# Where the split operands of a decoder layer begin within a 16-byte line of SBUF, and one projection made in half-width products

## The chip, the cores and the metric

The kernel runs on one core of a Trainium2 chip. The metric is the device time of one execution in microseconds; the kernel before takes 2354.44 us as the median of three runs (2353.5 to 2355.1). A forecast is compared with that median.

## The reference, cut to what matters

Sixteen batches of 512 tokens with 512 channels pass through one decoder layer, all in float32:

```
qkv = einsum('btc,ec->bte', x, Wqkv) + bqkv          # 512 -> 3 x 512
q, k = elu(q * scale) + 1, elu(k * scale) + 1
y = q * cumsum(k * v) / clip(einsum over a head(q, cumsum(k)), 0.001)
x = layernorm(x + y @ Wproj.T + bproj)
x = layernorm(x + channel_attention(x, ctx_1024))     # 4 heads of 128 channels, twice
e = argmax(mean over tokens(x) @ Wr + br)             # one expert of 8 per batch
h = relu(x @ W1[e] + b1[e])                           # 512 -> 2048
x = layernorm(x + h @ W2[e] + b2[e])                  # 2048 -> 512
```

## The kernel before

TensorE multiplies in the type float32r. To keep float32 accuracy, each float32 operand is split in SBUF into a high part (ScalarE copies it into a float32r tensor) and a low part (VectorE subtracts the high part from the original). A product of two matrices then takes three products: high by high, high by low, low by high. In each one operand is stationary (128 x 128, loaded by an LDWEIGHTS before every product) and the other moves past it (128 rows, 512 columns, 2048 bytes in each partition).

Four places make nearly all products:

- **The projections q, k and v** (`by_high` L1045 to L1049 and `qkv` L1051 to L1080). A batch has 12 jobs (3 kinds x 4 blocks of 128 channels). A job walks over the four channel tiles t of the input; at each t two products take xT_hi as moving operand (high and low weights, L1049) and one takes xT_lo (L1079). That makes 12 x 4 x 3 = 144 products for a batch, 2304 for all. Batch 1 uses x2T_hi and x2T_lo in place of xT_hi and xT_lo.
- **The output projection** (`project`, L1117 to L1119): 4 x 4 x 3 = 48 products for a batch. Here xT_hi and xT_lo (after the attention they hold y) are stationary and the weights wp_hi and wp_lo move.
- **The expert's first layer** (`up`, L1250 to L1252): for each of 16 blocks of the hidden width, 4 x 3 = 12 products into one PSUM bank. The weights we_hi and we_lo are stationary, x2T_hi and x2T_lo move: 192 products for a batch, 3072 for all.
- **The expert's second layer** (`down`, L1274, and for the last four blocks `down_last`, L1290): again 12 products for each block. The hidden parts h_hi and h_lo are stationary, the weights we_hi and we_lo move: 192 for a batch, 3072 for all.

The remaining products (the Gram matrix of x and the context, transposes, token sums) are plain float32 with 128 or fewer columns; they don't use the split tensors.

Each engine's order is fixed by a table of time slots: `JOB`, `DEN`, `FFN` and their like give for each step of the work the half-step at which an engine issues it. The batches overlap, so that projections and attention of later batches stand between the expert blocks of an earlier one. `up` of a block stands three half-steps ahead of its `down`; in between ScalarE makes hid and h_hi (L561, L568) and VectorE h_lo (L921). Semaphores, all written by hand, order the engines against each other.

In the beginning `qkv(0, 0, 0)` waits at each channel tile t for xhi_done and xlo_done, that is for ScalarE's xT_hi (L658) and VectorE's xT_lo (L1010) of that tile. Before it, `keep_busy` issues some products without a use.

All tensors are allocated one behind the other. In the built program each of them begins at a multiple of 16 bytes in its partition, and the slices that TensorE reads are multiples of 512 bytes into them, so that no operand of a product begins anywhere else than at the start of a 16-byte line. The lines that the change touches:

```
xT_hi, xT_lo = sb("xT_hi", [P, CC, T], F32R), sb("xT_lo", [P, CC, T], F32R)
x2T_hi, x2T_lo = sb("x2T_hi", [P, CC, T], F32R), sb("x2T_lo", [P, CC, T], F32R)
h_hi, h_lo = sb("h_hi", [P, 2, T], F32R), sb("h_lo", [P, 2, T], F32R)
```

h_hi has a second use: for batches 0 and 1 it holds the high and low weights of projection job 11, which SyncE also stores to DRAM once (L279).

Of the kernel before, what the change touches and what calls it, by code (L numbers as in the profile page):

```python
# [6 lines left out]
F32R = mybir.dt.float32r  # L7
# [5 lines left out]
P = 128  # L13
NB = 16
T = 512
C = 512
CC = C // P
# [82 lines left out]
def build(nc, d, out):  # L100
    wq_dram = nc.dram_tensor("wq_scratch", [JOBS, P, 2 * CC * P], F32, kind="Internal").ap()

    with ExitStack() as ctx:
        def sb(name, shape, dt=F32):
            return ctx.enter_context(nc.sbuf_tensor(name, shape, dt))
# [8 lines left out]
        raw_q = raw[:, :, :].rearrange("p r (s n) -> p (r s) n", s=2)  # L114
        diag = sb("diag", [P, 2, XH, P], F32R)
        xT_raw = sb("xT_raw", [P, CC, T])
        xT_hi, xT_lo = sb("xT_hi", [P, CC, T], F32R), sb("xT_lo", [P, CC, T], F32R)
        x2T_hi, x2T_lo = sb("x2T_hi", [P, CC, T], F32R), sb("x2T_lo", [P, CC, T], F32R)
        h_hi, h_lo = sb("h_hi", [P, 2, T], F32R), sb("h_lo", [P, 2, T], F32R)
        hid = sb("hid", [P, 2, T])  # L120
        rden_all = sb("rden_all", [P, T], F32R)
        head_all = sb("head_all", [P, CC, P], F32R)
# [10 lines left out]
        aT = sb("aT", [P, XH, P])  # L133
        const_b = sb("const_b", [P, C])
        x_sum = sb("x_sum", [P, C])

        ident, ones, ones_r = sb("ident", [P, P]), sb("ones", [P, P]), sb("ones_r", [P, P], F32R)
        head_sum = sb("head_sum", [P, CC, SEG])
# [79 lines left out]
        def bank(a, j):  # L218
            return (acc if a == 1 or a == 2 and j < EARLY else AB)[j % 2]
# [820 lines left out]
        def _(pe):  # L1040
            def keep_busy(bank, n):
                for _ in range(n):
                    pe.matmul(bank[:, 0:P], ones[:, :], ones[:, :], start=True, stop=True)

            def by_high(a, j, t):  # L1045
                w = held(j if a < 2 else j % NQ).rearrange("p (s t n) -> p s t n", s=2, t=CC)
                x_hi = x2T_hi if a == 1 else xT_hi
                for s in range(2):
                    pe.matmul(bank(a, j)[:, :], w[:, s, t, :], x_hi[:, t, :], start=(t == 0 and s == 0), stop=False)  # L1049

            def qkv(a, cc, part):  # L1051
                j = 3 * cc + part
                if a == 0:
                    pe.wait_ge(wqhi_done, j + 1)
                    pe.wait_ge(wqlo_done, j + 1)
                if a > 1:
                    pe.wait_ge(wq_in[j % NQ], 16 * (CC * (a - 2) + cc + 1))

                if part == 0 and cc > 0:
                    pe.wait_ge(kv_done, CC * a + cc)  # L1060
                if part == 1 and cc > 0:
                    pe.wait_ge(eq_done, 2 * CC * a + 2 * cc)
                if part == 2:
                    pe.wait_ge(ek_done, 2 * CC * a + 2 * cc + 2)
                if a == 2 and j < 2:
                    pe.wait_ge((kv_done, eq_done)[j], (2 * CC, 4 * CC)[j])
                n = j - EARLY if a == 2 else j
                if n in (0, 1) and a > 1:
                    pe.wait_ge(res1_done, TT * a - n)
                    pe.wait_ge(x2lo_done, CC * (a - 2) + 2 + n)  # L1070
                w = held(j if a < 2 else j % NQ).rearrange("p (s t n) -> p s t n", s=2, t=CC)
                x_lo = x2T_lo if a == 1 else xT_lo
                for t in range(CC):
                    if j == 0 and (a == 0 or t % 2 == 0):
                        pe.wait_ge(xhi_done, t + 1 if a == 0 else 2 * a + t // 2 + 3)
                        pe.wait_ge(xlo_done, t + 1 if a == 0 else 2 * a + t // 2 + 3)
                    if not ahead(a, j, t):
                        by_high(a, j, t)
                    last = pe.matmul(bank(a, j)[:, :], w[:, 0, t, :], x_lo[:, t, :], start=False, stop=(t == CC - 1))  # L1079
                last.then_inc(JOB_MM[part], 1)  # L1080

            def denominator(a):
# [333 lines left out]
```

## Time and profile before

| what | value |
|---|---|
| median of three runs | 2354.44 us (2353.5 to 2355.1) |
| profiled execution, first to last instruction (span) | 2352.2 us |
| TensorE busy with products | 2332.6 us, 99% |
| TensorE busy with weight loads (beside products) | 1927.6 us, 82% |
| VectorE busy | 1652.7 us, 70% |
| ScalarE busy | 1144.1 us, 49% |
| GpSimd busy | 451.6 us, 19% |
| mean granted clock of TensorE | 0.998 of full speed |

The span is the profiled execution's own time from its first to its last instruction; the page gives no other time for it. The median of the unprofiled runs lies 2.2 us above it, which covers what lies around the span and the spread from run to run.

How to read it: the products are pipelined, so the mean duration of one (389 ns for 512 columns) is not what it costs. What it costs is the distance from its start to the start of the next. A busy share of 99% therefore says that TensorE hardly ever ran dry, not that its products could not be closer together. The distance is read from the timeline, in which rows that have several products ("x2") begin with the first of them.

### The profile page before, as it was taken

Reading aid. Unit: us, or ns where it says so; the run is one execution under the profiler, and the core shown is the slowest. Engines: PE = TensorE matmul, PEld = TensorE weight load, DVE = VectorE, ACT = ScalarE, POOL = GpSimd, SP = SyncE. Lnnn points to the kernel's source line nnn. Section 1 sums busy time; section 2 is a strip of 40 time slices with the busy share of each in tenths; the row PEclk is TensorE's granted clock in tenths of the full one; section 3 lists DMA queues with packets and bytes.
Section 4 is the critical chain, followed back from the end, with each engine's and each line's share of the span. In section 5 each row is a group of like instructions: output and inputs, shape, how many; then the busy total and the mean of one; then the engine's idle time right before and its main releaser. Section 6 shows DMA issues by size and latency. Waiting matters only on the chain.

```text
span 2352.2 us, 34307 instructions
## 1 busy us (share of the span) xinstructions
PE 2332.6 (99%) x12060; PEld 1927.6 (82%) x12060; DVE 1652.7 (70%) x2863; ACT 1144.1 (49%) x1902; POOL 451.6 (19%) x395
## 2 busy tenths in 40 slices
PE   9999999999999999999999999999999999999998
PEld 7878888888888888888888888888888888888787
DVE  8886685866858668586675867758677586875643
ACT  5354445454454544545455444545454454554543
POOL 1112211121121212212122111211113111121200
PEclk9999999999999999999999999999999999999999
DMA  9255445463444634446354454544536435453332
GB/s 341 83 160 188 117 144 163 133 218 106 150 155 143 207 102 179 132 144 206 108 182 133 138 193 126 187 127 143 180 117 206 117 135 179 126 161 99 100 116 90
DMA packets 97276, 354.77 MB, mean 151 GB/s; under 512 B 11858, under 2 KB 11986, under 8 KB 86994
## 3 DMA queue, kind: packets, MB, share of 16 engines
q1 hardware_dynamic: 80210, 319.02, 38.2%
q0 software_dynamic: 16896, 33.56, 9.0%
q8 instruction: 98, 1.61, 0.3%
q14 instruction: 72, 0.59, 0.1%
HBM read 329.47 MB, written 23.07 MB: 150 GB/s over the span
## 4 chain that ended last, share of the span: by engine, by line
PE 92%; DVE 1%; ACT 1%; issue 1%; POOL 0%; DMA 0%; SPq 0%; POOLq 0%; DVEq 0%; ACTq 0%
PE acc L1274 29%; PE m L1049 13%; PE h_ps L1250 10%; PE h_ps L1252 10%; PE h_ps L1251 10%; PE m L1079 6%; PE m L1133 2%; PE m L1210 2%; PE m L1117 2%; PE m L1118 2%; PE m L1119 2%; PE m L1231 1%; PE m L1090 1%; PE m L1103 1%; PE acc L1290 0%
## 5 line engine op out<-in xcount | busy, mean ns | idle before, releaser
L561 ACT ACTIVATE hid<-h_ps,b 128x512 f32<-128x512 f32 x252 | 173.6, 689 | 598.2 <-PE h_ps L1252 597.5
L1049 PE MATMUL m<-xT_hi,wq 128*128 128x512 f32 x1320 | 408.2, 390 | 0.3 <-DVE xT_lo L1010 0.3
L1250 PE MATMUL h_ps<-x2T_hi,we_hi 128*128 128x512 f32 x1008 | 400.4, 397 | 2.4 <-DVE x2T_lo L905 2.4
L1274 PE MATMUL acc<-we_hi,h_hi 128*128 128x512 f32 x1008 | 400.8, 398 | 1.5 <-DVE h_lo L921 1.5
L921 DVE TENSOR_TENSOR h_lo<-hid,h_hi 128x512 fp32r<-128x512 f32 x252 | 224.3, 890 | 252.9 <-ACT h_hi L568 252.9
L1252 PE MATMUL h_ps<-x2T_hi,we_lo 128*128 128x512 f32 x1008 | 392.9, 390 | 0.0
L1274 PE MATMUL acc<-we_hi,h_lo 128*128 128x512 f32 x1008 | 392.8, 390 | 0.0
L1274 PE MATMUL acc<-we_lo,h_hi 128*128 128x512 f32 x1008 | 392.7, 390 | 0.0
L1251 PE MATMUL h_ps<-x2T_lo,we_hi 128*128 128x512 f32 x1008 | 392.4, 389 | 0.0
L911 DVE TENSOR_TENSOR we_lo<-raw,we_hi 128x1024 fp32r<-128x1024 f32 x256 | 319.9, 1250 | 31.2 <-ACT we_hi L551 31.2
L499 ACT ACTIVATE e_f<-m,sb_qkv,scale 128x512 f32<-128x512 f32 x116 | 90.5, 780 | 479.8 <-PE m L1079 477.7
L1049 PEld LDWEIGHTS m<-xT_hi,wq 128*128 128x128 f32 x1320 | 246.7, 188 | 51.3 <-ACT xT_hi L658 0.7
L551 ACT ACTIVATE we_hi<-raw 128x1024 fp32r<-128x1024 f32 x256 | 267.9, 1046 | 6.7 <-DMA raw<-in_w 6.3
L1079 PE MATMUL m<-xT_lo,wq 128*128 128x512 f32 x660 | 257.0, 389 | 0.0
L1250 PEld LDWEIGHTS h_ps<-x2T_hi,we_hi 128*128 128x128 f32 x1008 | 189.3, 188 | 43.5 <-issue 4.1
L1274 PEld LDWEIGHTS acc<-we_hi,h_hi 128*128 128x128 f32 x1008 | 189.4, 188 | 41.3 <-issue 3.0
L1274 PEld LDWEIGHTS acc<-we_hi,h_lo 128*128 128x128 f32 x1008 | 189.2, 188 | 40.3
L1252 PEld LDWEIGHTS h_ps<-x2T_hi,we_lo 128*128 128x128 f32 x1008 | 189.2, 188 | 40.2
L1251 PEld LDWEIGHTS h_ps<-x2T_lo,we_hi 128*128 128x128 f32 x1008 | 189.4, 188 | 37.1
L1274 PEld LDWEIGHTS acc<-we_lo,h_hi 128*128 128x128 f32 x1008 | 189.5, 188 | 36.8
L568 ACT ACTIVATE h_hi<-hid 128x512 fp32r<-128x512 f32 x252 | 159.5, 633 | 8.0
L1079 PEld LDWEIGHTS m<-xT_lo,wq 128*128 128x128 f32 x660 | 123.9, 188 | 26.0
(259 smaller groups left out, 3368.6 us busy)
## 6 DMA issues: line engine op xcount, KB each, us to landing
raw<-in_w SPq DMA_DIRECT2D x256, 512.0 KB, 4.2
wq<-wq_scratch SPq DMA_DIRECT2D x168, 512.0 KB, 3.3
x<-in_x_tok SPq DMA_DIRECT2D x16, 1024.0 KB, 5.5
x<-in_b_proj POOLq DMA_DIRECT2D x16, 1024.0 KB, 14.7
ctx_T<-in_ctxT SPq DMA_DIRECT2D x16, 1024.0 KB, 8.2
x<-in_b POOLq DMA_DIRECT2D x16, 1024.0 KB, 11.8
ctx_tok<-in_ctx_tok SPq DMA_DIRECT2D x15, 1024.0 KB, 4.7
out_dram<-x SPq DMA_DIRECT2D x15, 1024.0 KB, 4.8
```

The costliest lines, as they stand in the source:

```text
L499: act.activation(e_f[:, :], ps[:, :], ACT.Exp, bias=sb_qkv[:, col:col + 1], scale=scale[:, 0:1]).then_inc(done, 1)
L551: act.activation(we_hi[:, g % NW, :], raw[:, g % NR, :], ACT.Copy).then_inc(whi_done, 1)
L561: act.activation(hid[:, f % 2, :], up_bank(b, f)[:, :], ACT.Relu, bias=b1[:, b % 2, f:f + 1]).then_inc(h_done, 1)
L568: act.activation(h_part(h_hi, xT_hi, b, f), hid[:, f % 2, :], ACT.Copy).then_inc(hhi_done, 1)
L911: dve.tensor_tensor(we_lo[:, g % NW, :], raw[:, g % NR, :], we_hi[:, g % NW, :].bitcast(F32), ALU.subtract).then_inc(wlo_done, 1)
L921: dve.tensor_tensor(h_part(h_lo, xT_lo, b, f), hid[:, f % 2, :], h_part(h_hi, xT_hi, b, f).bitcast(F32), ALU.subtract).then_inc(hlo_done, 1)
L1049: pe.matmul(bank(a, j)[:, :], w[:, s, t, :], x_hi[:, t, :], start=(t == 0 and s == 0), stop=False)
L1079: last = pe.matmul(bank(a, j)[:, :], w[:, 0, t, :], x_lo[:, t, :], start=False, stop=(t == CC - 1))
L1250: pe.matmul(ps, we_hi[:, g % NW, js], x2T_hi[:, j, :], start=(j == 0), stop=False)
L1251: pe.matmul(ps, we_hi[:, g % NW, js], x2T_lo[:, j, :], start=False, stop=False)
L1252: last = pe.matmul(ps, we_lo[:, g % NW, js], x2T_hi[:, j, :], start=False, stop=(j == CC - 1))
L1274: last = pe.matmul(acc[t][:, :], hx[:, f % 2, ts], wx[:, g % NW, C:], start=(f == 0 and n == 0), stop=(f == FC - 1 and n == 2))
```

## The change

The six split tensors x2T, h and xT (high and low each) are no longer allocated by themselves. They are slices of one tensor `split` of 4 + 4 x 4 x 512 + 4 x 512 words in each partition, whose own start is a multiple of 16 bytes. x2T_hi and x2T_lo begin one word (4 bytes) past a 16-byte line, h_hi and h_lo two words (8 bytes), xT_hi and xT_lo three words (12 bytes). Every slice of them that an engine reads or writes keeps that offset, since all steps within them are multiples of 512 bytes. The tensors that stood behind them (from hid to x_sum) move down in the partition by multiples of 512 bytes; the small ones behind `split` move up by 32 bytes.

The second part: job 0 of batch 0 (`a == 0 and j == 0`) is made of products of 256 columns, two in place of each one of 512. That takes 24 products and 24 weight loads in place of 12.

```diff
-        xT_hi, xT_lo = sb("xT_hi", [P, CC, T], F32R), sb("xT_lo", [P, CC, T], F32R)
-        x2T_hi, x2T_lo = sb("x2T_hi", [P, CC, T], F32R), sb("x2T_lo", [P, CC, T], F32R)
-        h_hi, h_lo = sb("h_hi", [P, 2, T], F32R), sb("h_lo", [P, 2, T], F32R)
...
+        split = sb("split", [P, 4 + 4 * CC * T + 4 * T], F32R)
+
+        def part(words, n, tiles):
+            return split[:, words + n * tiles * T:words + (n + 1) * tiles * T].rearrange("p (c t) -> p c t", c=tiles)
+
+        x2T_hi, x2T_lo = part(1, 0, CC), part(1, 1, CC)
+        h_hi, h_lo = part(2 + 2 * CC * T, 0, 2), part(2 + 2 * CC * T, 1, 2)
+        xT_hi, xT_lo = part(3 + 2 * CC * T + 4 * T, 0, CC), part(3 + 2 * CC * T + 4 * T, 1, CC)
...
+            def columns(a, j):
+                return (slice(0, T // 2), slice(T // 2, T)) if a == 0 and j == 0 else (slice(0, T),)
+
             def by_high(a, j, t):
...
                 for s in range(2):
-                    pe.matmul(bank(a, j)[:, :], w[:, s, t, :], x_hi[:, t, :], start=(t == 0 and s == 0), stop=False)
+                    for n, ns in enumerate(columns(a, j)):
+                        pe.matmul(bank(a, j)[:, ns], w[:, s, t, :], x_hi[:, t, ns], start=(t == 0 and s == 0 and n == 0), stop=False)
...
-                    last = pe.matmul(bank(a, j)[:, :], w[:, 0, t, :], x_lo[:, t, :], start=False, stop=(t == CC - 1))
+                    for ns in columns(a, j):
+                        last = pe.matmul(bank(a, j)[:, ns], w[:, 0, t, :], x_lo[:, t, ns], start=False,
+                                         stop=(t == CC - 1 and ns.stop == T))
```

The order of instructions differs in one place only, on TensorE in the beginning of the program. Before, jobs 0 and 1 of batch 0 stand there so (m is the PSUM bank, wq the weights):

```order
L1043 MATMUL m<-ones 128x128
L1049 MATMUL m<-xT_hi,wq 128x512 x2
L1079 MATMUL m<-xT_lo,wq 128x512
L1049 MATMUL m<-xT_hi,wq 128x512 x2
L1079 MATMUL m<-xT_lo,wq 128x512
```

In the changed kernel the same place on TensorE reads so, where `split` is the tensor that holds all six parts:

```order
L1048 MATMUL m<-ones 128x128
L1058 MATMUL m<-split,wq 128x256 x4
L1089 MATMUL m<-split,wq 128x256 x2
L1058 MATMUL m<-split,wq 128x256 x4
L1089 MATMUL m<-split,wq 128x256 x2
L1058 MATMUL m<-split,wq 128x256 x4
L1089 MATMUL m<-split,wq 128x256 x2
L1058 MATMUL m<-split,wq 128x256 x4
L1089 MATMUL m<-split,wq 128x256 x2
L1058 MATMUL m<-split,wq 128x512 x2
L1089 MATMUL m<-split,wq 128x512
```

Each of the four channel tiles of job 0 has six products in place of three. From job 1 on (the last two rows), and on VectorE, ScalarE, GpSimd and SyncE throughout, as many instructions stand in the same order as before, with the same shapes.

## Rows read from the trace of the kernel before

**Rows 1.** The page: span, busy time by engine, chain that ended last.
```profile
span 2352.2 us, 34307 instructions
PE 2332.6 (99%) x12060; PEld 1927.6 (82%) x12060; DVE 1652.7 (70%) x2863; ACT 1144.1 (49%) x1902; POOL 451.6 (19%) x395
...
PE 92%; DVE 1%; ACT 1%; issue 1%; POOL 0%; DMA 0%; SPq 0%; POOLq 0%; DVEq 0%; ACTq 0%
```

**Rows 2.** Groups by form: count, busy us, mean ns, idle us before with releaser.
```profile
L1049 PE MATMUL m<-xT_hi,wq 128*128 128x512 f32 x1320 | 408.2, 390 | 0.3 <-DVE xT_lo L1010 0.3
L1274 PE MATMUL acc<-we_hi,h_hi 128*128 128x512 f32 x1008 | 400.8, 398 | 1.5 <-DVE h_lo L921 1.5
L1250 PE MATMUL h_ps<-x2T_hi,we_hi 128*128 128x512 f32 x1008 | 400.4, 397 | 2.4 <-DVE x2T_lo L905 2.4
...
L1251 PE MATMUL h_ps<-x2T_lo,we_hi 128*128 128x512 f32 x1008 | 392.4, 389 | 0.0
```

**Rows 3.** Timeline of TensorE (start us, us, instruction), projections of batch 0.
```profile
16.18 0.61 PE L1049 MATMUL m<-xT_hi,we_hi 128*128 128x512 f32 x2
...
36.58 0.61 PE L1049 MATMUL m<-xT_hi,we_lo 128*128 128x512 f32 x2
```

**Rows 4.** Timeline of TensorE in the middle: Gram, a second and a first expert layer.
```profile
1001.20 3.73 PE L1133 MATMUL m<-ctx_tok,x 128*128 128x128 f32 x32
...
1005.46 0.39 PE L1274 MATMUL acc<-we_hi,h_hi 128*128 128x512 f32 x1
...
1007.28 0.39 PE L1274 MATMUL acc<-we_hi,h_lo 128*128 128x512 f32 x1
...
1010.22 0.39 PE L1250 MATMUL h_ps<-x2T_hi,we_hi 128*128 128x512 f32 x1
...
1011.81 0.39 PE L1251 MATMUL h_ps<-x2T_lo,we_hi 128*128 128x512 f32 x1
```

**Rows 5.** By stretch: us, busy of PE, PEld, DVE, ACT, POOL; granted clock.
```profile
40.00:47.80 7.80, 5.91 (x53) 4.28 (x51) 7.64 (x11) 4.17 (x6) 0.00 (x0) 1.00 1.07 265
47.80:54.60 6.80, 6.09 (x12) 3.77 (x13) 6.78 (x11) 5.22 (x10) 0.00 (x0) 0.50 0.96 399
```

**Rows 6.** Timeline of TensorE within that second stretch.
```profile
48.16 1.22 PE L1103 MATMUL m<-rden_all,head_all 128*128 128x512 f32 x2 [2.25 <-ACT rden_all L627]
...
53.39 0.63 PE L1118 MATMUL m<-wp_lo,xT_hi 128*128 128x512 f32 x1
53.81 0.63 PE L1119 MATMUL m<-wp_hi,xT_lo 128*128 128x512 f32 x1
```

**Rows 7.** Weight loads by form.
```profile
L1133 PEld LDWEIGHTS m<-ctx_tok,x 128*128 128x128 f32 x480 | 55.9, 192 | 1.2
...
L1250 PEld LDWEIGHTS h_ps<-x2T_hi,we_hi 128*128 128x128 f32 x1008 | 189.3, 188 | 43.5 <-issue 4.1 <-DVE x2T_lo L905 1.7
```

**Rows 8.** Timeline of TensorE, job 0 and the beginning of job 1.
```profile
6.50 0.86 PE L1049 MATMUL m<-xT_hi,wq 128*128 128x512 f32 x2
...
7.44 0.62 PE L1049 MATMUL m<-xT_hi,wq 128*128 128x512 f32 x2
...
8.59 0.70 PE L1049 MATMUL m<-xT_hi,wq 128*128 128x512 f32 x2 [0.30 <-DVE xT_lo L1010]
...
10.04 0.62 PE L1049 MATMUL m<-xT_hi,wq 128*128 128x512 f32 x2
```

**Rows 9.** Groups of VectorE and ScalarE that write the split tensors.
```profile
L921 DVE TENSOR_TENSOR h_lo<-hid,h_hi 128x512 fp32r<-128x512 f32 x252 | 224.3, 890 | 252.9 <-ACT h_hi L568 252.9
L905 DVE TENSOR_TENSOR x2T_lo<-m,x2T_hi 128x512 fp32r<-128x512 f32 x62 | 40.0, 685 | 61.6 <-ACT x2T_hi L540 61.6
L753 DVE TENSOR_TENSOR xT_lo<-ctx_tok,xT_hi 128x512 fp32r<-128x512 f32 x60 | 38.5, 686 | 20.9 <-ACT xT_hi L522 20.9
...
L568 ACT ACTIVATE h_hi<-hid 128x512 fp32r<-128x512 f32 x252 | 159.5, 633 | 8.0
```

## The prediction

> **What bounds the kernel now.** I read the page first: of a span of 2352.2 us TensorE is busy for 2332.6, and the chain that ended last lies on it for 92% [rows 1]. The groups by form come next, to see what TensorE ever waits for: the first product of a block in the expert's first layer was late by 2.4 us in all, that of the second layer by 1.5 us, that of the projections by 0.3 us [rows 2]. So there is nearly no wait to remove, and no other engine's time matters unless it grows a lot. What counts is the distance between the starts of products.
>
> That distance is in the timeline. From 16.18 to 36.58 us there are thirty groups of three products without a gap: 20.40 / 90 = 0.2267 us for one product of 512 columns [rows 3]. The middle of the program has the same: 8 distances in 1.82 us in the second layer and 7 in 1.59 us in the first, 0.227 us each [rows 4]. At 2.4 GHz 512 columns are 213.3 ns. Each product thus costs 13.3 ns more than its columns (32 cycles), whichever stage it stands in and whatever the others do meanwhile. In a stretch with the clock granted at half, 1.2 GHz [rows 5], the distance is 53.81 - 53.39 = 0.42 us [rows 6], and 512 columns at 1.2 GHz are 426.7 ns: there the extra is gone. So the 13.3 ns don't look like a fixed price of an instruction, but like something that shows only when words are wanted at the full rate. Loading weights doesn't set the distance: a load takes 188 ns and is hidden, with 43.5 us of idle time before the 1008 loads of one group, and in the Gram matrix 32 products, each with a load of its own, stand (3.73 - 0.27) / 31 = 0.112 us apart, the last one's own length of about 0.27 us taken off [rows 4, 7].
>
> **The change, part by part.** *Where the moving operand begins.* xT and x2T move in the projections (12 jobs x 4 tiles x 3 products x 16 batches = 2304) and in the first expert layer (16 blocks x 12 x 16 = 3072): 5376 products whose 2048 bytes begin 4 or 12 bytes past a line and so touch 129 lines where 128 were touched. The second expert layer and the output projection move weights, which stay where they were. In the trace every operand begins at a line, so the price of the offset stands nowhere and needs bounds. Upper end: the stream falls to one word for each cycle at 1.2 GHz, the 426.7 ns that the half clock shows [rows 6], which is 200 ns more for each, 5376 x 0.2 = 1075 us. Lower end: the offset takes away what makes the 13.3 ns, 5376 x 13.3 ns = 72 us less. Between them lies one more line: 213.3 ns for 128 lines are 1.67 ns a line, and 226.7 / 128 = 1.77 ns; at most 5376 x 1.77 = 9.5 us. I take nothing for it. The nearest row to an uneven stream is a product at the full clock, and its distance is the same in all stages although the weight slices and the work of ScalarE and VectorE beside it vary; the reading seems to be fetched ahead, and one fetch more at the ends of 512 columns can fall into the 13.3 ns between them.
>
> On this point there is a rule that speaks against the change. The Trainium skill, page "SBUF — State Buffer", section "Specifications (TRN2)", says that SBUF is read in lines of 16 bytes, that two hits on a line are needed for the full rate and that each step to a new line costs something. A product that begins 12 bytes past a line has one hit on its first line, one that begins 4 bytes past it has one hit on its last. No row here shows it. If the rule holds as a price for each line, the sum is the +9 us of the first rival below; if it is only about single hits, it is less.
>
> *Where the stationary operand begins.* h is stationary in the second expert layer (3072) and xT or x2T in the output projection (48 x 16 = 768); h_hi as weights of job 11 adds 24. A load reads 512 bytes, 33 lines in place of 32. It ends 227 - 188 = 39 ns ahead of the next one's start [rows 3, 7], so it could become a fifth longer unseen: nothing. Were that cover gone, 3864 loads at one line each (at most 188 / 32 = 5.9 ns) would be 23 us. Below nothing, if the 13.3 ns came from loads that meet the moving stream: a further 3864 x 13.3 ns = 51 us less.
>
> *VectorE and ScalarE.* They write all six parts and VectorE reads the high ones again. Their durations now are 633 to 890 ns [rows 9]. VectorE's mean for h_lo is 890 ns where the same operation takes 685 for x2T_lo [rows 9]; so it is already drawn out by 0.2 us in the mean, and TensorE has waited only 1.5 us for it in 2352 [rows 2]. An odd start that cost a few cycles, or even again 0.2 us, is hidden behind the three half-steps between the two expert layers: nothing. The lower bound is nothing too, since faster helpers shorten no wait above 4.2 us in all (2.4 + 1.5 + 0.3). If the cover were gone, with 0.2 us for each of the 256 h_lo exposed, it would be 51 us; the engine is busy for 70% only, and I don't see it.
>
> *Halves in job 0 of batch 0.* 12 products become 24. One of 256 columns takes at least half of 226.7 ns, 113.3, which is also about the 112 ns at which products with their own load follow each other [rows 4]; at most as long as a whole one, 226.7. With a fixed 13.3 ns it would be 120, and this I take: 24 x 120 - 12 x 226.7 = +160 ns, with ends of 0 and +2.7 us. A part of it lies beside a wait: at 8.59 us TensorE stands 0.30 us for VectorE's xT_lo, and the first tiles are apart by 7.44 - 6.50 and 8.59 - 7.44 us, more than three products need [rows 8]. Behind the third tile TensorE doesn't wait again until job 1 at 10.04 us, so only two tiles' extra of 80 ns moves what follows. Queued behind are the jobs of batch 0, and VectorE and ScalarE wait for those, not the reverse.
>
> *Sum* against the profiled execution: 2352.2 + 0 + 0 + 0 + 0.1 = 2352.3 us of span. The median of the runs is 2.2 us above the span, which gives 2354.5. As several of the small prices above can only add, and hardly one of them is negative, I forecast 2355. The case's own range is 2353 to 2358.
>
> **The rivals.**
> 1. *An extra line is paid.* This is the case on the other side, slower: one mechanism, in the projections and the first expert layer, at the seam between two products. If TensorE's reading of a stream is bound by lines (1.77 ns each at 226.7 / 128), 129 lines cost 228.4 ns, and 5376 x 1.77 = +9.5 us: 2364. It decides once the price is above 0.9 ns for a product (4.7 us). For it: the extra shows only at the full clock, so the stream does run at its limit there [rows 3, 6]. Against: 32 cycles between products would be room for one fetch. With half a line, 0.8 ns, it would be +4.5 us: 2359, at the edge.
> 2. *The stream loses its rate.* If the words are fetched in pairs or fours that must not cross a line, and a crossing one takes twice: 226.7 ns becomes between 320 (half of the fetches double) and 427 ns, + 0.5 to 1.1 ms: 2860 to 3430. For it: at 2.4 GHz a word each 0.42 ns has to come, twice the rate at which the half clock asks for words [rows 6]. Against: nothing in the trace, as no operand is off its line; I hold a fetch by whole lines to be likelier.
> 3. *The extra of 13.3 ns goes away.* If it comes from stationary and moving operand beginning at the same place of a line, then all 9216 products with a part of `split` gain it: 2354 - 9216 x 13.3 ns = 2232; if for the moving ones alone, 2283. For it: the extra vanishes at the half clock, where both streams ask for less [rows 6], and every product pairs one shifted operand with one at a line. Against: 4 to 12 bytes keep both streams in nearly the same lines, and the extra is the same over all slices of the weights [rows 3, 4].
>    The Trainium skill, page "TensorE: Matmul & The Clock Gate", section "Part 2: What happens when you issue a matmul", gives TensorE two read ports that don't disturb each other, which would exclude this rival; it also gives a distance of N / 2.4 + 2.5 ns, 216 ns for 512 columns, and there the trace differs: 226.7.
> 4. *The clock.* TensorE idled 2.25 us for rden_all up to 48.16, and the clock stood at half from 47.8 to 54.6, with 6.09 us of work in it [rows 5, 6]. Should the shift of 0.1 us at the start move that stretch, up to half of the work, 3 us, comes or goes. It is inside the range.
>
> **How the numbers follow.** No change: 0.48. Rival 1: 0.26, a third of it below the point at which it can be told. Rival 2: 0.12. Rival 3: 0.09. The clock and mixtures: 0.05. What a measurement of this kernel can tell from no change is about 0.2%, 4.7 us. Within it: 0.48 + 0.09 + 0.01 = 0.58. Slower: 0.17 + 0.12 + 0.03 = 0.32. Faster: 0.09 + 0.01 = 0.10. The time is that of the likeliest case, 2355. The range leaves out rival 2 and most of rival 3, together 0.2; it holds rival 1 with some of a longer load on top, up to 2372, and a partial gain (a tenth of rival 3) down to 2342.
>
> **What would show it.** In the timeline of the changed kernel: products of the first expert layer and of the projections 226.7 ns apart as before (right), 228 (rival 1), over 300 (rival 2), about 214 (rival 3). The second expert layer keeps 226.7 ns in every case but rival 3, and its loads 188 ns. The 24 products of job 0 should stand 120 ns apart once the third tile has begun; 113 would say that the extra goes with the columns. VectorE's h_lo may be longer, but TensorE's idle time before the expert layers should stay below 5 us. The forecast is wrong if any distance of 512-column products changes by more than 0.9 ns.

## The result, and the profile after: slower by 2%

The changed kernel takes 2401.15 us (median of 4 runs, 2400.22 to 2401.72), the kernel before 2354.44 beside it (median of three, 2353.5 to 2355.1): a ratio of 1.0199, with a 95% interval of 1.0185 to 1.0214. A fourth execution of the kernel before took 8350.22 us and is left out of this comparison. The changed kernel is clearly slower; the interval leaves open whether by a little more or a little less than 2%. The forecast was 2355 us, with a range of 2342 to 2372. So 46 us have come that it did not see. The page of the profile after [rows 1]:

```profile
span 2399.1 us, 34331 instructions
PE 2379.6 (99%) x12072; PEld 1934.9 (81%) x12072; DVE 1651.1 (69%) x2863; ACT 1143.7 (48%) x1902; POOL 452.2 (19%) x395
...
PE 96%; DVE 2%; ACT 1%; issue 1%; POOL 0%; DMA 0%; SPq 0%; POOLq 0%; DVEq 0%; ACTq 0%
```

The span grew by 46.9 us and TensorE's busy time by 47.0, with 12 products and 12 loads more. VectorE and ScalarE have kept their sums to within 2 us. TensorE is "99% busy" as before: from this page alone the loss can't be told from work. The groups of the profile after (count, busy us, mean ns, idle us before them) answer to [rows 2, 7, 9]:

```profile
L1261 PE MATMUL h_ps<-split,we_hi 128*128 128x512 f32 x1008 | 410.3, 407 | 2.2 <-DVE split L910 2.2
L1058 PE MATMUL m<-split,wq 128*128 128x512 f32 x1312 | 408.4, 392 | 0.0
L1262 PE MATMUL h_ps<-split,we_hi 128*128 128x512 f32 x1008 | 402.3, 399 | 0.0
L1285 PE MATMUL acc<-we_lo,split 128*128 128x512 f32 x1008 | 395.7, 393 | 0.0
...
L1261 PEld LDWEIGHTS h_ps<-split,we_hi 128*128 128x128 f32 x1008 | 189.7, 188 | 49.8 <-issue 4.0
...
L926 DVE TENSOR_TENSOR split<-hid,split 128x512 fp32r<-128x512 f32 x256 | 224.0, 875 | 283.6 <-ACT split L573 283.6
```

TensorE waited 2.2 us for VectorE in the first expert layer where it had waited 2.4, h_lo takes 875 ns where it took 890, the loads take 188 ns as before. What grew is one product: 407 and 399 ns in the first layer (397 and 389 before), 393 in the second, where the group of we_lo and h_hi had 390. The distances behind that are in the timeline (start us, us, instruction) of the kernel after, in the middle of the program, beside [rows 4]:

```profile
1016.07 0.40 PE L1261 MATMUL h_ps<-split,we_hi 128*128 128x512 f32 x1
...
1017.50 0.64 PE L1058 MATMUL m<-split,wq 128*128 128x512 f32 x2
...
1024.07 0.39 PE L1285 MATMUL acc<-we_lo,split 128*128 128x512 f32 x1
...
1026.37 0.39 PE L1285 MATMUL acc<-we_hi,split 128*128 128x512 f32 x1
...
1029.34 0.40 PE L1261 MATMUL h_ps<-split,we_hi 128*128 128x512 f32 x1
...
1032.18 0.40 PE L1152 MATMUL m<-diag,ones_r 128*128 128x512 f32 x1
```

Six products of the first layer lie between 1016.07 and 1017.50: 0.238 us each, and twelve between 1029.34 and 1032.18: 0.237. Ten distances of the second layer lie between 1024.07 and 1026.37: 0.230. Before they were 0.227 in both [rows 4]. In the projections of batch 0 (timeline of the kernel after, against [rows 3]) it is 60 products in 13.73 us, 0.2288 us each:

```profile
16.20 0.62 PE L1058 MATMUL m<-split,we_hi 128*128 128x512 f32 x2
...
29.93 0.62 PE L1058 MATMUL m<-split,we_lo 128*128 128x512 f32 x2
```

The table below is worked out from all pairs of consecutive starts in each trace that lie under 262 ns apart (some 9000 a trace); the experiments' kernels are told below. Mean distance in ns:

| kernel | first expert layer | second | projections | output projection | ratio to before (95%) |
|---|---|---|---|---|---|
| before | 227.3 | 227.4 | 227.1 | 226.7 | |
| after | 237.2 | 230.8 | 229.8 | 228.6 | 1.0199 |
| e2_place | 227.4 | 227.6 | 227.0 | 226.8 | 1.0005 (0.9996 to 1.0015) |
| e3_x2_only | 237.9 | 228.7 | 228.3 | 228.0 | 1.0162 (1.0145 to 1.0179) |
| e4_h_only | 227.7 | 231.0 | 227.2 | 226.8 | 1.0050 (1.0033 to 1.0066) |
| e6_x_only | 228.1 | 227.8 | 229.3 | 227.2 | 1.0042 (1.0025 to 1.0059) |
| e7_whole_line | 231.5 | 228.5 | 228.0 | 228.1 | 1.0079 (1.0062 to 1.0096) |
| e8_halves_only | 227.5 | 227.6 | 227.0 | 226.8 | 1.0006 (0.9996 to 1.0015) |
| e10_x2_256_bytes | 227.3 | 227.5 | 227.0 | 226.8 | 1.0000 (0.9991 to 1.0010) |
| e11_h_36_words | 227.4 | 228.7 | 227.5 | 226.8 | 1.0026 (1.0016 to 1.0036) |
| e12_all_36_words | 232.1 | 232.2 | 233.1 | 226.9 | 1.0180 (1.0166 to 1.0194) |

The second row against the first accounts for the loss: 3072 x 9.9 ns = 30.4 us in the first layer, 3072 x 3.4 = 10.4 in the second, 2304 x 2.7 = 6.2 in the projections, 768 x 1.9 = 1.5 in the output projection, together 48.5. Two small things of these two executions stand beside it. TensorE waited 0.91 us for the third tile of job 0 and began it at 9.22 us, where it had been 8.59 [rows 8]: +0.6. The half-width products alone don't do this: in e8 that tile began at 8.57 us. And less was done at the half clock, by the windows of the profile after (columns as in [rows 5]):

```profile
51.20:54.60 3.40, 3.30 (x8) 2.21 (x8) 3.40 (x7) 2.80 (x7) 0.00 (x0) 0.50 0.59 248
```

TensorE worked 3.30 us at half speed where it had been 6.09 [rows 5]: that gives back half of 2.8, 1.4 us. The sum is 47.7 against 46.9 of span.

### The profile page after: what moved, and what is told of

The parts are those of the page before. It is cut to its first block, busy times and chain, and to the rows that moved or that the text cites. A ratio compares the mean times of both kernels' runs of the same rounds, so it can differ in the third digit from the quotient of the medians.

```text
span 2399.1 us, 34331 instructions
## 1 busy us (share of the span) xinstructions
PE 2379.6 (99%) x12072; PEld 1934.9 (81%) x12072; DVE 1651.1 (69%) x2863; ACT 1143.7 (48%) x1902; POOL 452.2 (19%) x395
## 4 chain that ended last, share of the span: by engine, by line
PE 96%; DVE 2%; ACT 1%; issue 1%; POOL 0%; DMA 0%; SPq 0%; POOLq 0%; DVEq 0%; ACTq 0%
PE acc L1285 28%; PE m L1058 13%; PE h_ps L1261 10%; PE h_ps L1263 10%; PE h_ps L1262 10%; PE m L1089 7%; PE m L1128 2%; PE m L1129 2%; PE m L1130 2%; PE m L1144 2%; PE m L1221 2%; PE m L1242 1%; PE acc L1058 1%; PE m L1101 1%; PE m L1114 1%
## 5 line engine op out<-in xcount | busy, mean ns | idle before, releaser
L1285 PE MATMUL acc<-we_hi,split 128*128 128x512 f32 x2016 | 677.9, 397 | 1.2 <-DVE split L926 1.2
L1285 PEld LDWEIGHTS acc<-we_hi,split 128*128 128x128 f32 x2016 | 379.1, 188 | 87.2 <-issue 3.0
L926 DVE TENSOR_TENSOR split<-hid,split 128x512 fp32r<-128x512 f32 x256 | 224.0, 875 | 283.6 <-ACT split L573 283.6
L1261 PE MATMUL h_ps<-split,we_hi 128*128 128x512 f32 x1008 | 410.3, 407 | 2.2 <-DVE split L910 2.2
L1058 PE MATMUL m<-split,wq 128*128 128x512 f32 (+1 forms) x1328 | 411.2, 391 | 0.9 <-DVE split L1015 0.9
L1263 PE MATMUL h_ps<-split,we_lo 128*128 128x512 f32 x1008 | 402.7, 399 | 0.0
L1262 PE MATMUL h_ps<-split,we_hi 128*128 128x512 f32 x1008 | 402.3, 399 | 0.0
L1285 PE MATMUL acc<-we_lo,split 128*128 128x512 f32 x1008 | 395.7, 393 | 0.0
L1058 PEld LDWEIGHTS m<-split,wq 128*128 128x128 f32 x1328 | 247.6, 188 | 55.5 <-ACT split L663 1.1
L1089 PE MATMUL m<-split,wq 128*128 128x512 f32 (+1 forms) x664 | 257.5, 389 | 0.0
L1261 PEld LDWEIGHTS h_ps<-split,we_hi 128*128 128x128 f32 x1008 | 189.7, 188 | 49.8 <-issue 4.0
L1263 PEld LDWEIGHTS h_ps<-split,we_lo 128*128 128x128 f32 x1008 | 191.3, 190 | 47.2
L1262 PEld LDWEIGHTS h_ps<-split,we_hi 128*128 128x128 f32 x1008 | 192.0, 190 | 44.1
L1089 PEld LDWEIGHTS m<-split,wq 128*128 128x128 f32 x664 | 124.3, 188 | 27.5
L522 ACT ACTIVATE x<-x,shift,rstd 128x512 f32<-128x512 f32 x188 | 138.0, 809 | 13.3 <-POOL shift L409 10.1
## 6 DMA issues: line engine op xcount, KB each, us to landing
x<-in_b POOLq DMA_DIRECT2D x16, 1024.0 KB, 11.8
```

Source lines behind the costliest of these rows:

```text
L522: act.activation(x[:, t, :], x[:, t, :], ACT.Identity, bias=shift[:, n, t:t + 1], scale=rstd[:, n, t:t + 1]).then_inc((x1_done, x2_done, n ...
L926: dve.tensor_tensor(h_part(h_lo, xT_lo, b, f), hid[:, f % 2, :], h_part(h_hi, xT_hi, b, f).bitcast(F32), ALU.subtract).then_inc(hlo_done, 1)
L1058: pe.matmul(bank(a, j)[:, ns], w[:, s, t, :], x_hi[:, t, ns], start=(t == 0 and s == 0 and n == 0), stop=False)
L1089: last = pe.matmul(bank(a, j)[:, ns], w[:, 0, t, :], x_lo[:, t, ns], start=False, stop=(t == CC - 1 and ns.stop == T))
L1261: pe.matmul(ps, we_hi[:, g % NW, js], x2T_hi[:, j, :], start=(j == 0), stop=False)
L1262: pe.matmul(ps, we_hi[:, g % NW, js], x2T_lo[:, j, :], start=False, stop=False)
```

## The experiments

All whole kernels are the changed kernel with other places for the parts and, but for e8, with job 0 in whole products, unless said otherwise, and every ratio is to the kernel before, run beside it on the same chip (2354.1 to 2354.4 us). e1, e5 and e9 leave the layer out and are one execution each. The expectations speak of three theories: a product pays where its own operand begins within a 16-byte line, and shifts by whole lines are free (A); the place of one operand against the other counts (B); the traffic of ScalarE and VectorE beside TensorE is needed (C).

**e1_pairs: both operands' offsets by themselves.** The layer is left out; TensorE alone does blocks of 32 products like the kernel's, each block with its own pair of offsets in words (m for the moving, s for the stationary operand), a plain product between blocks:

```
pe.matmul(bank[:, 0:n], still[:, s + j * P:s + j * P + P], moving[:, m + j * T:m + j * T + n], ...)   # j = i // 3 % 4
```

> Leaves the whole layer out (the output is a copy of x). TensorE alone: blocks of 32 float32r products, each with its own weight load, nothing beside them. The start of the moving operand and that of the stationary one are stepped through 0, 1, 2, 3, 4, 5, 6 and 8 words, all 64 pairs, and then 16, 32, 64 words for one of them, then 256 and 384 columns. Theory A (a price for each product that begins within a 16-byte line): 226.7 ns where both begin at 0, 4 or 8 words, about 237 ns where the moving operand is 1 word off, about 229 where it is 3 off, and 230 where the stationary one is 2 off. Theory B (the distance of the two streams decides, since the weights of the next product are read while this one moves): equal shifts of both (1,1), (2,2), (3,3) cost nothing, and shifts by whole lines (4, 8, 16 words of one of them) cost as well. Theory C (it needs the traffic of ScalarE and VectorE on the same tensors): all 64 pairs at 226.7 ns. For 256 columns a fixed extra gives 120 ns, an extra for each column 113 ns.

Measured: 588.34 us in all. The timeline of TensorE gives each block's length; s is 0, and m is 0, 1, 2, 3, 4, 5, 6, 8. Behind the first gap stand (m, s) = (4, 1), (4, 4) and (8, 4), behind the last one (0, 32) and (0, 64):

```profile
18.80 7.54 PE L62 MATMUL b<-moving,still 128*128 128x512 f32 x32
26.32 7.84 PE L62 MATMUL b<-moving,still 128*128 128x512 f32 x32
34.13 7.72 PE L62 MATMUL b<-moving,still 128*128 128x512 f32 x32
41.83 7.58 PE L62 MATMUL b<-moving,still 128*128 128x512 f32 x32
49.39 7.66 PE L62 MATMUL b<-moving,still 128*128 128x512 f32 x32
57.02 7.88 PE L62 MATMUL b<-moving,still 128*128 128x512 f32 x32
64.88 7.73 PE L62 MATMUL b<-moving,still 128*128 128x512 f32 x32
72.59 7.70 PE L62 MATMUL b<-moving,still 128*128 128x512 f32 x32
...
111.10 7.52 PE L62 MATMUL b<-moving,still 128*128 128x512 f32 x32
...
295.38 7.61 PE L62 MATMUL b<-moving,still 128*128 128x512 f32 x32
...
318.49 7.55 PE L62 MATMUL b<-moving,still 128*128 128x512 f32 x32
...
541.29 7.69 PE L62 MATMUL b<-moving,still 128*128 128x512 f32 x32
548.96 7.53 PE L62 MATMUL b<-moving,still 128*128 128x512 f32 x32
```

One word costs 0.30 us for 30 distances, 10 ns each, with VectorE, ScalarE and GpSimd idle: C falls, their traffic isn't needed for the price. Four and eight words are whole lines and cost 0.12 and 0.16 us: A's claim that they are free falls. On the stationary side 32 words cost about as much as 8 on the moving one, and 64 words (256 bytes) nothing. The starts within the blocks (the first distance of a block, some 315 ns, left out) give, in ns: 226.7 for (0, 0) once it has settled, 237.4 for (1, 0), 233.9 for (2, 0), 229.1 for (3, 0), 231.7 for (4, 0); 232.4, 230.7, 233.3 and 233.4 for (0, 1), (0, 2), (0, 3), (0, 4). Equal shifts aren't free: (1, 1) has 237.9, (2, 2) 233.1, (3, 3) 229.2 and (4, 4), where both operands begin at a line, 230.0; only (8, 8) settles back at 226.7. So B in its plain form falls too. Two unequal pairs settle at 226.6 all the same: (4, 1) and (8, 4).

**e2_place: the new tensor without any offset.**

```
+ x2T_hi, x2T_lo = part(0, 0, CC), part(0, 1, CC)
+ h_hi, h_lo = part(8 * T, 0, 2), part(8 * T, 1, 2)
+ xT_hi, xT_lo = part(12 * T, 0, CC), part(12 * T, 1, CC)
+ return (slice(0, T),)        # columns(): no halves
```

> The one tensor split as in the change, at the same place, but with all three pairs of parts at 0 words, and job 0 in whole products. Theory A (begin within a line): as before, 2354 us. Theory B (distance of the two streams): as before too, but for the few products with ones_r, which stays 32 bytes further on and should stay at 234 ns in place of 227. Rival (the place in the partition, not the offset): 2400 us as in the change.

Measured: 2355.72 us (2354.11 to 2357.22), ratio 1.0005 (0.9996 to 1.0015). One tensor for six and another layout cost nothing that can be told.

One small thing doesn't come back. The products of ones_r with diag and of head_all with rden_all are float32r with 512 columns too, which the account ahead of the prediction passes over. ones_r (stationary) stands 32 bytes further on here, as in the changed kernel, and diag (moving) doesn't. Within the 15 pairs of such products that stood at L1190 and L1191, one start follows the other by 226.8 ns in the kernel before, 230.9 here, and 226.9 in e10, where ones_r has moved by a multiple of 256 bytes. The expectation said 234. There are 64 such products, under 0.3 us in all.

**e3_x2_only: of the offsets only x2's 4 bytes.** As e2, with h at 0, x at 4 * T words, and

```
+ x2T_hi, x2T_lo = part(1 + 12 * T, 0, CC), part(1 + 12 * T, 1, CC)
```

> Only x2T_hi and x2T_lo begin one word past a line, h and x at a line, job 0 in whole products. By the distances in the trace of the changed kernel: 3072 products of the first expert layer at 237 ns in place of 226.7, and 144 projections of batch 1, +33 us: 2387 us. If the price came from VectorE or ScalarE, TensorE would show idle time before the expert layers instead, and its distances would stay 226.7.

Measured: 2392.87 us, ratio 1.0162 (1.0145 to 1.0179): +38 us of the 46. The group by form of this kernel's first layer reads like that of the kernel after:

```profile
L1261 PE MATMUL h_ps<-split,we_hi 128*128 128x512 f32 x1008 | 410.4, 407 | 2.3 <-DVE split L910 2.3
```

3072 x 10.6 ns are 32.6 us. The 144 projections of batch 1, which read x2, stand at 236.5 ns, 1.4 us more. The rest lies in stages whose operands weren't moved: the second layer at 228.7 ns, the projections of the other batches at 227.8, the output projection at 228.0. They take turns with the shifted ones.

**e4_h_only: only h's 8 bytes, the stationary operand.**

```
+ h_hi, h_lo = part(2 + 16 * T, 0, 2), part(2 + 16 * T, 1, 2)
```

> Only h_hi and h_lo begin two words past a line. They are stationary in the second expert layer. If a stationary operand off its line costs by itself: 3072 products at 230.7 in place of 226.7 ns, +12 us: 2366 us. If the 230.7 ns in the changed kernel were a consequence of x2 and x beside them (products with both operands at a line stood 231 apart there too): 2354 us.

Measured: 2365.86 us, ratio 1.0050 (1.0033 to 1.0066), +11.5 us, and the second layer alone has moved: 231.0 ns, x 3072 = 11.1 us. Its groups:

```profile
L1285 PE MATMUL acc<-we_hi,split 128*128 128x512 f32 x2016 | 678.4, 397 | 1.4 <-DVE split L926 1.4
...
L1262 PE MATMUL h_ps<-split,we_hi 128*128 128x512 f32 x1008 | 392.9, 390 | 0.0
```

**e5_loads: narrower loads, coarser shifts.** The layer is left out as in e1, with blocks of 48 products; the stationary operand has 128, 64 or 32 columns, then the shifts go by whole lines up to 60 words.

```
- pe.matmul(bank[:, 0:n], still[:, s + j * P:s + j * P + P], ...)
+ pe.matmul(bank[0:cols, 0:n], still[:, s + j * P:s + j * P + cols], ...)
```

> Leaves the layer out, as the first study of pairs did; blocks of 48 products of 512 columns. First the width of the stationary operand: 128, 64, 32 columns, each with the moving one at 0, 1, 2, 3 words. Then one of the two shifted by 4, 8, ... 60 words (whole lines), then both by 8, 16, 32, then the moving one at 1 with the stationary one further on. Theory B (the stream of a product and the load of the next product's weights get in each other's way, by their distance): with 32 columns a load reads a quarter, so the cost of a shift falls to about a quarter (from 10.5 to under 4 ns at 1 word), and shifts by whole lines cost 2 to 7 ns except where the distance is a multiple of 64 words; equal shifts of both return to 226.7. Theory A (a price of the product's own begin within a line): the 10.5, 7 and 2.5 ns at 1, 2, 3 words stay whatever the width, and whole lines cost nothing. The fixed 13.3 ns: if it comes from loading weights it shrinks with the width, towards 217 ns; if it is TensorE's own, it stays.

Measured: 626.66 us in all. Timeline of TensorE: offsets (0, 0) and (1, 0) at 128 columns, (0, 0) at 64, then (0, 36) and (8, 8) at 128:

```profile
20.41 11.16 PE L62 MATMUL b<-moving,still 128*128 128x512 f32 x48
31.55 11.64 PE L62 MATMUL b<-moving,still 128*128 128x512 f32 x48
...
65.82 11.28 PE L62 MATMUL b<-moving,still 128*64 128x512 f32 x48
...
418.87 11.13 PE L62 MATMUL b<-moving,still 128*128 128x512 f32 x48
...
497.83 11.16 PE L62 MATMUL b<-moving,still 128*128 128x512 f32 x48
```

A load of half the width doesn't bring the distance down: 230.0 ns at m = 0 and 237.2 at m = 1, and 231.7 and 236.1 with 32 columns. So the 13.3 ns aren't the length of the load. The width isn't without effect, though. The difference between m = 1 and m = 0 goes from 11.2 to 7.2 and 4.4 ns, mostly because the distance at m = 0 grows, and m = 2, at 233.3 ns with 128 columns, has 230.0 with 64 and with 32. B's share in this stays undecided. By whole lines (one operand moved by 4 to 60 words, the other not) 29 of 30 places cost 1.6 to 10 ns, most of them near 6.7; only 36 words on the stationary side come back to 226.7. Both operands moved by 8, 16 or 32 words alike give 226.7. With m at 1 word none of eight places of the stationary operand helps (236.1 to 240.0). So two things count: the moving operand's word within its line, and how the two operands lie to each other, this with a period of 64 words. They aren't the whole. (0, 0) and (4, 4) agree in both and stand at 226.7 and 230.0 in e1; (4, 0) and (8, 4) agree in both and stand at 231.7 and 226.6. Of the equal shifts tried, only those by a multiple of 8 words came back to 226.7.

**e6_x_only: only x's 12 bytes.**

```
+ xT_hi, xT_lo = part(3 + 12 * T, 0, CC), part(3 + 12 * T, 1, CC)
```

> Only xT_hi and xT_lo begin three words past a line. They move in 2160 projections and are stationary in 768 products of the output projection. By the distances in the changed kernel (229.8 and 228.6 ns): +2.8 x 2160 + 1.9 x 768 = +7.5 us, 2362 us. The three single shifts so far (+38.5 for x2, +11.5 for h) already make more than the whole change (+46.8); if prices simply added, x would have to be at -3 us: 2351 us.

Measured: 2363.42 us, ratio 1.0042 (1.0025 to 1.0059), +9.3 us. 2304 x 2.2 ns = 5.1 us are in the projections, 768 x 0.5 = 0.4 in the output projection, the others in the two expert layers, whose operands weren't moved.

**e7_whole_line: x2 at 16 bytes.** Every operand begins at a line, as before; only its distance to the others has changed.

```
+ x2T_hi, x2T_lo = part(4 + 12 * T, 0, CC), part(4 + 12 * T, 1, CC)
```

> As the run with x2 alone, but x2T_hi and x2T_lo begin four words, one whole line, further on, so every product of the kernel begins at a line. Theory A (begin within a line): 2354 us. Theory B (distance of the stream and the load beside it): the first expert layer at about 232 ns, as the pair of 4 and 0 words measured, +5 x 3072 = +16 us: 2370 us.

Measured: 2372.45 us, ratio 1.0079 (1.0062 to 1.0096), +18 us. Its first layer:

```profile
L1261 PE MATMUL h_ps<-split,we_hi 128*128 128x512 f32 x1008 | 404.0, 401 | 2.3 <-DVE split L910 2.3
```

401 ns, between the 397 of [rows 2] and the 407 of the kernel after. No line more is read than before, so theory A can't be the whole of it. This run decides it in the kernel.

**e8_halves_only: no offsets, the halves kept.**

```
+ x2T_hi, x2T_lo = part(0, 0, CC), part(0, 1, CC)        # h and x as in e2
```

> The layout with all parts at 0 words, and job 0 of batch 0 in products of 256 columns: the other part of the change alone. 24 products at 120 ns in place of 12 at 226.7, of which the first half lies beside waits: 0 to +0.2 us, 2354 to 2355 us; by time alone the same as before.

Measured: 2355.30 us, ratio 1.0006 (0.9996 to 1.0015): nothing, as forecast.

**e9_columns: what the price goes with.** The layer is left out; blocks of 48 products of n columns, moving operand at 0 to 3 words, stationary at 0.

```
+ PAIRS = [(m, 0, n, 128) for n in (512, 510, 508, 504, 496, ..., 256) for m in range(4)]
```

> Leaves the layer out; blocks of 48 products alone with the stationary operand at a line and the moving one at 0, 1, 2, 3 words, for 512, 510, 508, 504, 496, 480, 448, 416, 384, 352, 320 and 256 columns. If the odd start is paid through the extra line, 508 or 510 columns at 1 word (128 lines again, or 129 with less in them) bring the cost down by steps with the lines touched, and it is about the same 10 ns for every width that touches one line more. If it is paid in the gap between two products (the distances seen so far are the columns plus 32, 48 or 64 cycles of 2.4 GHz), the cost depends on the width by jumps and is zero for some widths, as it was for 384 columns.

Timeline of TensorE: m = 0 and 1 at 512 columns, then at 508, then at 504:

```profile
19.70 11.17 PE L59 MATMUL b<-moving,still 128*128 128x512 f32 x48
30.84 11.64 PE L59 MATMUL b<-moving,still 128*128 128x512 f32 x48
...
110.24 11.16 PE L59 MATMUL b<-moving,still 128*128 128x508 f32 x48
121.39 11.44 PE L59 MATMUL b<-moving,still 128*128 128x508 f32 x48
...
155.33 11.13 PE L59 MATMUL b<-moving,still 128*128 128x504 f32 x48
166.44 11.12 PE L59 MATMUL b<-moving,still 128*128 128x504 f32 x48
```

One word costs 0.47 us for 46 distances at 512 columns (10 ns), 0.28 at 508 and nothing at 504, although there too one line more is touched than at 0. And 512, 508 and 504 columns take the same time at 0. Distances in ns, settled:

| columns | m = 0 | 1 | 2 | 3 |
|---|---|---|---|---|
| 512 | 226.7 | 237.7 | 233.3 | 228.9 |
| 504 | 226.7 | 226.7 | 226.7 | 226.7 |
| 448 | 202.6 | 206.7 | 206.7 | 200.0 |
| 384 | 173.3 | 173.3 | 180.0 | 173.3 |
| 320 | 146.7 | 153.3 | 146.7 | 146.7 |
| 256 | 120.0 | 123.3 | 126.7 | 116.7 |

With 448 and with 256 columns, 3 words are even faster than 0. At 2.4 GHz 226.7, 233.3 and 240 ns are 544, 560 and 576 cycles: steps of 16. That what lies between is a mean over a pattern of them is a guess. So the price is neither one for each line nor one for each column.

**e10_x2_256_bytes: x2 at 64 words.**

```
+ x2T_hi, x2T_lo = part(64 + 12 * T, 0, CC), part(64 + 12 * T, 1, CC)
```

> As the run with x2 one line further on, but x2T_hi and x2T_lo begin 64 words (256 bytes) further on. In the study of pairs a distance of 64 words between the two operands took 226.7 ns as 0 did. Theory B (distance of the two operands, with a period of 256 bytes): as before, 2354 to 2356 us. If any displacement costs, or the room that split takes: 2370 us as with the whole line.

Measured: 2354.50 us, ratio 1.0000 (0.9991 to 1.0010), with the first layer back:

```profile
L1261 PE MATMUL h_ps<-split,we_hi 128*128 128x512 f32 x1008 | 400.4, 397 | 2.3 <-DVE split L910 2.3
```

The price has a period of 256 bytes in the kernel too. In the kernel before, the tensors up to ones_r have sizes that are multiples of 256 bytes and stand one behind the other, so they stand alike modulo 256 bytes, and none paid.

**e11_h_36_words and e12_all_36_words: is there a better place?** Stationary at 36 words was the one other place that settled at 226.7 in e5. Both are the kernel before, with h moved; e12 moves wq and the stationary half of we_hi and we_lo as well. Moving operands and the output projection stay where they were.

```
- h_hi, h_lo = sb("h_hi", [P, 2, T], F32R), sb("h_lo", [P, 2, T], F32R)
+ OFF = 36
+ h_hi, h_lo = (sb(n, [P, 2 * T + 64], F32R)[:, OFF:OFF + 2 * T].rearrange("p (f t) -> p f t", f=2) for n in ("h_hi", "h_lo"))
+ wq = sb("wq", [P, NQ * 2 * C + 64], F32R)[:, OFF:OFF + NQ * 2 * C].rearrange(...)     # e12 only, and we_hi, we_lo alike
```

> The kernel before, but h_hi and h_lo begin 36 words further on, the one distance of the stationary operand at which blocks stood at 226.7 ns from the second product on. Second expert layer: 226.7 in place of 227.4 ns, -2 us. If that holds in the kernel and the first expert layer keeps its distance: 2352 us. If the change of distance from stage to stage disturbs the neighbours, as in the other runs: 2356 to 2360 us.

> The kernel before, with all stationary operands of the projections and both expert layers (wq, the first halves of we_hi and we_lo, h_hi and h_lo) 36 words further on, and all moving ones as they were. If the products lock at once: about 0.5 ns less for each of 8400, -4 us, 2350 us, which would be faster than the kernel before by 0.2%. If the distance of 36 words is good only for the block's own pattern: 2354 to 2370 us.

Measured: e11 2360.78 us, ratio 1.0026 (1.0016 to 1.0036); e12 2396.79 us, ratio 1.0180 (1.0166 to 1.0194), with 232 to 233 ns in the projections and both expert layers, and 226.9 in the output projection. Both missed: e11 lies above its 2356 to 2360 us and e12 far above its 2354 to 2370. The place that was free by itself isn't in the kernel, and the turns that the stages take aren't the reason. In batch 0 of e12 the projections run without another stage between them, each with its stationary operand at 36 words:

```profile
16.23 0.63 PE L1056 MATMUL m<-xT_hi,we_hi 128*128 128x512 f32 x2
...
36.53 0.63 PE L1056 MATMUL m<-xT_hi,we_lo 128*128 128x512 f32 x2
```

That is 87 distances in 20.30 us, 233.3 ns each, where the block of e5 has 226.7. The output projection is a second place where the blocks don't foretell the kernel: with the stationary operand at 3 words e1 has 233.3 ns, e6 227.2 and the changed kernel 228.6. No version tried beats the kernel before.

## Why the prediction was wrong, by its steps

*What bounds the kernel* held: TensorE's distances, and nothing else, set the time, and all of the loss is in them.

*Where the moving operand begins* is the step that failed: "one fetch more at the ends of 512 columns can fall into the 13.3 ns between them". It took nothing for 5376 products; measured are 9.9 ns in 3072 of them and 2.7 ns in 2304, 36.6 us together, and e3 shows 38 us for x2 alone, neighbours included. The fault is in the reasoning: an equal distance in all stages was read as room that could swallow an uneven start. But every stage of the kernel before has the same offsets, so the equality said nothing about what happens at others. The bounds (-72 to +1075 us) held the value, and the range was cut far inside them on an argument that no row carried.

*Where the stationary operand begins* failed too, with the same fault in small. The cover of 39 ns behind the load is there, and the load keeps its 188 ns; yet the second layer lost 3.4 ns a product, in e4 3.6 (+11.5 us), and the output projection 1.9. The cost comes while the load keeps its length, which the step had taken as the only way. The check "the second expert layer keeps 226.7 ns in every case but rival 3" fell with it.

*Rival 1* had the right side and the wrong mechanism. It gave 1.77 ns for a line more and 2364 us. Measured are 36.6 us in the stages that it speaks of, nearly four times as much, with a price that differs among offsets that touch equally many lines (10.7 ns for 1 word and 2.4 for 3 in e1; 10.6 in e3 and 2.2 in e6) and that also comes where no line more is touched (e7, +4.2 ns) and stays away where one is (504 columns in e9). By the Trainium skill, page "SBUF — State Buffer", section "Specifications (TRN2)", reads go by lines of 16 bytes and want two hits on each. These runs agree in that the word within a line matters; the rule gives neither the whole line's 18 us nor the period of 256 bytes.

*Rivals 2 and 3* didn't come: at the full clock no block or stage of 512 columns has a settled mean above 240.1 ns or below 226.6. For rival 3 e1 tried equal shifts of both operands, and they cost up to 11 ns. Against it the prediction cited the Trainium skill's page "TensorE: Matmul & The Clock Gate", section "Part 2: What happens when you issue a matmul": two ports that don't disturb each other. The conclusion held, but these runs don't bear out the reason, since the distance does depend on where the one operand stands against the other (e5, e7).

*VectorE and ScalarE*, at nothing: right, with 2.2 and 1.2 us of wait before the expert layers, 875 ns for h_lo and e2 at 1.0005. *Halves*, at +0.1 us: right. In the timeline of the kernel after, six products of 256 columns lie between the first two rows, 117 ns each. 120 was forecast, and 120 is what the like products have in e8 without offsets; the 117 go with the 3 words of xT (116.7 in e9):

```profile
10.00 0.63 PE L1058 MATMUL m<-split,wq 128*128 128x256 f32 x4
...
10.70 0.62 PE L1058 MATMUL m<-split,wq 128*128 128x512 f32 x2
```

*The clock* came inside its term: 1.4 us given back where up to 3 were allowed.

*What the single runs don't add up to.* e3, e4 and e6 are +38.5, +11.5 and +9.3 us, 59 together, where the changed kernel has 46. In each single run the neighbours of the shifted stage pay as well. By the table the first layer loses 10.6 + 0.4 + 0.8 = 11.8 ns in the three single runs and 9.9 in the changed kernel, the second 1.3 + 3.6 + 0.4 = 5.3 and 3.4: 3072 x (1.9 + 1.9) = 11.7 of the 12.5 us. That a stage with a shift of its own doesn't pay a second time for its neighbours is argued from these sums. That neighbours pay is shown once more by e12: there ones_r and diag stand as before modulo 256 bytes, and their pairs went from 226.8 to 232.6 ns. In the changed kernel these pairs have 233.6, of which e2 shows 230.9 without any offset in `split`.

*What stays open.* It is shown that the distance follows the moving operand's word within its line and how the two operands lie to each other, with a period of 256 bytes; that the price is there with the other engines idle; and that neither the count of lines nor the length of the load gives it. The rule isn't complete: (0, 0) and (4, 4) differ in e1. Why it goes in steps of 16 cycles, why 1 word costs more than 3, and why 36 words are free alone and not in the kernel isn't settled by any run here. The blocks differ from the kernel in more than one thing: they use each pair of slices three times running, and no other engine works beside them.

## What to carry to other kernels

Where TensorE is the bound, let all float32r operands, moving and stationary, stand multiples of 256 bytes apart and without an offset of their own, as in the kernel before and in e10, and check it in the layout whenever a tensor is added or merged. The same offset on both sides isn't enough: in e1 (1, 1) has 237.9 ns and (4, 4) 230.0. Read the distance between starts in the timeline, not the busy share: "99% busy" held 2% of stalls here. And where all rows of a profile share one value of a quantity, they say nothing of its price: keep the bounds, and weigh them.

## What the runs showed of the hardware that was not expected

- The settled distance of float32r products with a load each has steps: 544 cycles for 504 to 512 columns, up to 560 or 576 with an unfavourable start; 120.0 ns at 256 columns, 173.3 at 384.
- Whole lines aren't neutral: 16 bytes cost 4.2 ns a product in the kernel (e7), 256 bytes nothing (e10).
- At the half clock the offset cost nothing. Four products of batch 1 with x2T_lo as moving operand fell into that stretch in both kernels, at a line before and 4 bytes past one after (timeline of before, then of after), and took 1.91 us each time, 427 ns from start to start:

```profile
50.93 1.91 PE L1079 MATMUL acc<-x2T_lo,wq 128*128 128x512 f32 x4
```

```profile
51.92 1.91 PE L1089 MATMUL acc<-split,wq 128*128 128x512 f32 x4
```

- Even with all operands alike, products can begin with longer distances and find back to the usual one. In the timeline of the kernel before, five distances lie in the first 1.15 us (230 to 236 ns, one of 229), and the next eight in 1.82 us (227):

```profile
1012.95 0.39 PE L1141 MATMUL m<-diag,ones_r 128*128 128x512 f32 x1
...
1014.10 0.39 PE L1274 MATMUL acc<-we_hi,h_hi 128*128 128x512 f32 x1
...
1015.92 0.39 PE L1274 MATMUL acc<-we_hi,h_lo 128*128 128x512 f32 x1
```
